# Two interleaved streams of one transformer program: their common order read from a table of runs

## What is computed

```python
x = L0_attn_hidden                                   # (4, 1024, 128)
x = layernorm(x + attn(x))          # global latent attention, then local attention, 16 heads of 8, 4 kv heads
x = layernorm(x + moe(x))           # 8 experts 128 -> 512 -> 128 (gelu), softmax gate, the 2 best
x = layernorm(x + linear_attn(x))   # elu + 1 feature maps of 64, running sum over the tokens
x = layernorm(x + local_layers(x))  # 2 layers: windows of 64 keys with 8 heads of 64, then a gated ffn (gelu)

# attn
x = x + global_latent_attn(rmsnorm(x, norm1_w), ...)   # rope and q/k norm, causal softmax over 1024
x = x + local_gqa_attn(rmsnorm(x, norm2_w), ...)       # window of 32

# local_layers, twice
h = shift_token(x); q, k, v = split(h @ wqkv)
q, k = rotary_xpos(l2norm(q) * qs, l2norm(k) * ks)
x = x + local_attention(q, k, v) @ wo
h = layernorm(shift_token(x)) * lg + lb
a, g = split(h @ w1 + b1); x = x + (a * gelu(g)) @ w2 + b2
```

## Time and profile before

| | us |
|---|---|
| median of 3 runs | 2644.71 |
| lowest, highest | 2635.4, 2645.03 |
| profiled execution | 2645.18 |
| its span | 2643.1 |
| mean granted clock of PE | 0.845 |

### The profile page before, as it was taken

How to read it: one execution, slowest core, us unless ns; L and a number is a source line. 1 busy time by engine, 2 the same in 40 slices (tenths; PEclk the granted TensorE clock), 3 DMA queues, 4 the chain that set the end, 5 groups by cost and what they waited for, 6 DMA issues and landing times.

```text
span 2643.1 us, 38819 instructions
## 1 busy us (share of the span) xinstructions
PE 2017.8 (76%) x14843; PEld 1256.7 (48%) x14843; DVE 1314.4 (50%) x2660; ACT 1241.3 (47%) x2610; POOL 592.8 (22%) x505
## 2 busy tenths in 40 slices
PE   2865986489867987679868976788757999758776
PEld 1123664244344755333545754442345666535454
DVE  4134225654366145445654157734665545467574
ACT  2642421376644331667543333566645565235453
POOL 0420000263311001235400011433510221024231
PEclk8776995698978986888888987888978999778998
DMA  3000000000000100000000000000100110000000
GB/s 112 1 1 1 25 25 1 10 16 10 25 5 17 41 13 5 5 13 17 25 14 16 33 9 9 13 5 17 33 5 5 33 33 17 0 20 21 13 17 13
DMA packets 32059, 45.50 MB, mean 17 GB/s; under 512 B 7824, under 2 KB 18948, under 8 KB 31748
## 3 DMA queue, kind: packets, MB, share of 16 engines
q1 hardware_dynamic: 31875, 43.01, 6.0%
HBM read 24.12 MB, written 2.10 MB: 10 GB/s over the span
## 4 chain that ended last, share of the span: by engine, by line
PE 53%; DVE 25%; ACT 10%; issue 7%; POOL 4%; SPq 1%; DVEq 0%; DMA 0%; ACTq 0%; POOLq 0%
PE PH L933 8%; PE PD L893 8%; PE PH L716 5%; PE PB L1082 4%; PE PB L1102 4%; PE PB L1018 3%; ACT back_arena L1345 2%; PE PD L760 2%; PE PB L1039 2%; PE PB L1138 2%; POOL front_arena L1936 2%; ACT front_arena L1213 2%; DVE back_arena L1818 2%; DVE back_arena L1817 1%; PE PB L1029 1%
## 5 line engine op out<-in xcount | busy, mean ns | idle before, releaser
L1973 POOL TENSOR_TENSOR back_arena<-back_arena 128x512 f32<-128x512 f32 x128 | 165.4, 1294 | 1052.3 <-DVE back_arena L1818 1052.2
L1213 ACT ACTIVATE front_arena<-PD 128x1024 f32<-128x1024 f32 (+3 forms) x384 | 303.3, 817 | 160.7 <-PE PD L760 159.0
L1302 ACT ACTIVATE front_arena<-PD,b 128x512 f32<-128x512 f32 x256 | 161.6, 683 | 260.6 <-PE PD L893 260.4
L933 PEld LDWEIGHTS PH<-W,front_arena 128*128 128x128 f32 x2048 | 248.2, 192 | 65.6 <-issue 34.1
L1936 POOL TENSOR_TENSOR front_arena<-front_arena,tri 128x256 f32<-128x256 f32 x256 | 201.1, 798 | 322.4 <-ACT front_arena L1213 321.6
L933 PE MATMUL PH<-W,front_arena 128*128 128x128 f32 x2048 | 255.3, 276 | 7.6 <-DVE R L1664 6.7
L1082 PE MATMUL PB<-wqkv,hT 128*128 128x512 f32 x384 | 233.1, 696 | 32.5 <-DVE back_arena L1818 12.7
L893 PE MATMUL PD<-xT,W 128*128 128x512 f32 x512 | 246.4, 605 | 1.2 <-ACT xT L1196 1.2
L716 PE MATMUL PH<-front_arena 128*32 128x512 f32 (+3 forms) x1536 | 189.4, 569 | 66.2 <-POOL front_arena L1936 41.5
L1825 DVE TENSOR_REDUCE fnm<-PB 128x4 f32<-128x512 f32 x128 | 88.3, 691 | 303.6 <-PE PB L1102 302.0
L1345 ACT ACTIVATE back_arena<-PB,fnm 128x128 f32<-128x128 f32 x512 | 180.9, 371 | 111.0 <-DVE fnm L1825 110.8
(11 more groups left out here) (241 smaller groups left out, 3398.0 us busy)
## 6 DMA issues: line engine op xcount, KB each, us to landing
W<-in_W SPq DMA_DIRECT2D x32, 512.0 KB, 3.4
back_arena<-back_arena SPq DMA_DIRECT2D x128, 128.0 KB, 2.3
X<-in_L_attn_hidden SPq DMA_DIRECT2D x64, 32.0 KB, 1.8
out_y<-Nb SPq DMA_DIRECT2D x64, 32.0 KB, 1.6
wqkv<-in_L_ffn_wqkv SPq DMA_DIRECT2D x1, 1536.0 KB
back_arena<-in_c_xpos SPq DMA_DIRECT2D x1, 1024.0 KB
back_arena<-in_L_ffn_w SPq DMA_DIRECT2D x1, 682.0 KB
wo<-in_L_ffn_wo SPq DMA_DIRECT2D x1, 512.0 KB
```

The lines of the kernel that those rows point to most:

```text
L933: ins = pe.matmul(p[:, 128 * t:128 * t + 128], hv[:, c, 128 * t:128 * t + 128], W12[e % WRING][:, HF + 128 * c:HF + 128 * c + 128], start= ...
L1213: act.activation(pb[:, :, 0:n], p[:, :, 0:n], ACT.Exp, scale=INV_SQRT_HD).then_inc(freed(b, "S", half, g, kc, jp), 1)
L1973: pool.tensor_tensor(T1[k % 2][:, hs, :], T1[k % 2][:, hs, :], T2[:, hs, :], ALU.add).then_inc(sg("rot"), 1)
```

## The change

The plan in `order()` is replaced by a table of run lengths, `RUNS`: 601 numbers for front, back, front and so on in turn, whose sums are the same 4 x 282 and 4 x 211 steps. The numbers were found offline by a search over the instructions and waits of the whole program. The estimates in the labels are no longer read. The first number is 283 and the last 223: front 0 is followed by one step of front 1 before back 0 starts, and the last 12 steps of back 2 stand ahead of back 3. The second edit puts `link(ins)`, which belongs to the last rotation product of `rope`, ahead of the yield of `qn` 0 instead of behind it.

```diff
--- before.py
+++ after.py
@@ -251,47 +251,28 @@
 assert len(F_AT) == len(FRONT) and len(B_AT) == len(BACK)
 
 
+RUNS = """
+283 1 8 2 3 1 3 1 2 1 3 2 3 1 4 1 9 1 1 1 2 1 4 1 10 1 1 2 2 2 1 1 1 3 2 2 1 1 1 7 2 2 2 1 1 4 1 1 1 1 1 3 1 5 2 5 3 1 1 1 1 1 1 2 1 16 2 1 1 2 1 2 1
...
+1 1 1 1 1 1 1 1 223
+"""
+
+
 def order():
 
-    streams = {"F": FRONT, "B": BACK}
-    left = {who: [sum(c[1] for _, c in labels[i:]) for i in range(len(labels))] for who, labels in streams.items()}
-    at, ready, out = {"F": 0, "B": 0}, {"F": 0.0, "B": 0.0}, []
-    pe = act = dve = 0.0
-    front_ends, taken = {}, {}
-    while at["F"] < B * len(FRONT) or at["B"] < B * len(BACK):
-        options = []
-        for who, labels in streams.items():
-            b, i = divmod(at[who], len(labels))
-            if b == B:
-                continue
-            start = ready[who]
-            if who == "B" and i == 0:
-                if b not in front_ends:
-                    continue
-                start = max(start, front_ends[b])
-            if who == "F" and i == 0 and b >= 2:
-                if b - 2 not in taken:
-                    continue
-                start = max(start, taken[b - 2])
-            (p, _, a, v) = labels[i][1]
-            start = max(start, pe if p else 0, act - 3, dve - 3)
-            behind = left[who][i] + (B - 1 - b) * left[who][0] + (left["B"][0] if who == "F" else 0)
-            options.append((start, -behind, who))
-        soonest = min(o[0] for o in options)
-        start, _, who = min((o for o in options if o[0] <= soonest + 0.05), key=lambda o: o[1])
-        b, i = divmod(at[who], len(streams[who]))
-        p, d, a, v = streams[who][i][1]
-        out.append((who, at[who]))
-        at[who] += 1
-        ready[who] = start + d
-        if p:
-            pe = start + p
-        act = max(act, start + p) + a if a else act
-        dve = max(dve, start + p) + v if v else dve
-        if who == "F" and i == len(FRONT) - 1:
-            front_ends[b] = ready[who]
-        if who == "B" and i == 0:
-            taken[b] = ready[who]
+    at, out = {"F": 0, "B": 0}, []
+    for n, run in enumerate(RUNS.split()):
+        who = "FB"[n % 2]
+        for _ in range(int(run)):
+            out.append((who, at[who]))
+            at[who] += 1
+    assert at == {"F": B * len(FRONT), "B": B * len(BACK)}, at
     return out
 
 
@@ -1533,8 +1514,8 @@
                         for s in range(2):
                             ins = dve.tensor_tensor(tmp[:, t, :, :, s], sw[:, t, :, :, 1 - s],
                                                     rope[a][:, t, 1:2, :].rearrange("p o (d s) -> p o d s", s=2)[:, :, :, s].to_broadcast([128, nh, HD // 2]), ALU.mult)
+                    link(ins)
                     yield front_at(b, "qn", a, 0)
-                    link(ins)
                     link(dve.tensor_tensor(QR, QR, arena_rope, ALU.add))
                     link(dve.tensor_tensor(arena_rope, QR, QR, ALU.mult))
                     yield front_at(b, "qn", a, 1)
```

## The result

| | before | after |
|---|---|---|
| median | 2644.87 | 2604.17 |
| lowest, highest | 2635.4, 2645.21 | 2595.42, 2604.94 |
| profiled execution | 2645.18 | 2595.42 |
| its span | 2643.1 | 2593.5 |
| mean granted clock of PE | 0.845 | 0.846 |

The ratio is 0.9847, interval [0.9817, 0.9877]: 41 us faster. Measured again beside other kernels the medians were 2598.65 and 2650.05, ratio 0.9804 [0.9785, 0.9823], 51 us. So 40 to 50 us is the size, and the forecast had 18.

The account below looks back on a forecast made before the run. Only the 1874 us middle, where PE idles 387 us, could change; DVE's strand limits the chain windows. 2645.2 - 5 (chain windows) - 8 (tables) - 5 (single waits) = 2627 us; ends 2607 to 2665, case range 2610 to 2644.

Parts of the forecast that it names:

- The middle part: Fronts 1 to 3 beside backs 0 to 2, 1874 us before: forecast some 1856, wrong if outside 1839 to 1873.
- The ends: Front 0 alone (467 us) and back 3 alone (302 us): same steps in both orders, so unchanged.
- The chain windows, what arrives: Last projection to `qT` (L854): some 58 back steps arrive, three windows grow by 47.6 (DVE alone) to 74 us.
- The chain windows, what leaves: Those 58 steps leave places costing 0.98 us each, 57 us; net of arrivals -5, ends -9 and +17.
- The tables: ScalarE's table loads fall from 82 to 69, 16.7 us of ACT; half taken, -8, bounds 0 and -17.
- Single waits: Waits outside the chain windows, such as before `nF` and `toT`, change: together -5 us, ends -12 and +3.
- The link: `link(ins)` above the yield makes DVE wait for the last rotation product: eight times nothing, at most 3 us.
- Unmixing: Rival: back steps in runs of four or more cost up to 1.28 us against 0.98 mixed; 2675 us, chance 0.18.
- Small waits go too: Rival: the new order also removes uncounted PE waits, such as at L716 behind the masks; 2575 us, chance 0.27.

Follow-up runs that it names:

- smooth_att: The changed kernel with back steps spread evenly in the six halves of global attention, hidden layers in one piece; 2642.6 us, 0.9991 of before.
- undo_dg: The changed kernel with the old order in the two pieces bringing 46 back steps into fronts 2 and 3's local chain windows; 2610.44 us, 0.9856 of before.
- tables_only: The old order with `link(ins)` moved and each back hidden layer's steps drawn together, 67 table loads instead of 82; 2658.57 us, 1.0051 of before.
- coarse: The new order's number of back steps between some 50 marks, spread evenly between them; 2689.8 us, 1.0162 of before.
- the filled kernels: The changed and the old kernel with PE's long idle pieces filled to the end by 857 and 1080 constant products; 2568.42 and 2599.74 us.
- part_a: The old order with `link(ins)` moved and the new order only from front 1's `toT` to its first local scores; 2637.86 us, 0.998 of before.
- part_bc: Old order, `link(ins)` moved, new order only from front 1's first local scores to half 1 of front 2's global attention; 2624.82 us, 0.9937 of before.
- part_dg: Old order, `link(ins)` moved, new order only in two pieces, from fronts 2 and 3's global attention into their local layers; 2644.19 us, 0.9991 of before.
- link_only: The old order with only the `link(ins)` line moved; 2642.76 us, 0.9988 of before.
- the two filled versions of before: The old kernel with constant products in PE's idle pieces: 773 (0.7 of each piece), 2636.27 us; 1080 (to the end), 2599.74 us.
- after_warm: The changed kernel with 641 products of a constant filling 0.7 of each long PE idle piece; 2593.85 us, 0.9779 of before.
- after_again: The changed kernel measured once more, nothing altered; 2598.65 us, 0.9804 of before.

## Why the prediction was right or wrong

Forecast 2627, measured 2604 and 2599: the direction and the range held, the size didn't. The middle part was to be between 1839 and 1873 us; it is 1820.7, so by its own test the forecast was wrong. **The step that failed** is the price of what leaves global attention: the mean of 0.98 us a step, with the places of the steps that stay put at nothing. Attention became 79.4 us shorter for 54 steps fewer, 1.47 each, and 48 of these us go when the same counts are spread evenly (smooth_att: 15 us of idle time, 33 us of PE busy longer at a lower clock). Step by step:

- **The ends.** Right in their order, wrong in "unchanged": back 3 alone took 307.3 instead of 299.1 us with the same instructions.
- **The chain windows, what arrives.** Right. Three windows were to get 58 steps and grow by 47.6 (DVE alone) to 74 us. They grew from 35.9, 38.6 and 38.3 to 44.1, 63.4 and 51.8, by 46.5: DVE's bound, 0.80 us a step. The forecast's -5 had taken 52 us, 0.90 a step. Idle time before `qT` was to fall under 8 us in fronts 2 and 3 local: it is 13.0 and 2.7. The other three windows changed by -12, +10 and -10 us.
- **The chain windows, what leaves.** This step failed. I priced a step that leaves attention at the *mean* of 0.92 to 1.04 us, and so had -57 against +48 to +55. In the whole order the six windows and the three attentions together became 45.0 us shorter (34.4 - 79.4). undo_dg shows what the two pieces did: 60 steps left attention and 67.3 us with them, 1.12 each (1.44 in front 2, 0.91 in front 3), and 53.7 us came elsewhere, 0.90 each. For this part alone, with 46 of the term's 58 steps, the term of -5 measures -6 to -14, mostly outside its end of -9. So the mean was not far off for these pieces; the large price belongs to the whole order with its places.
- **The tables.** The term of -8 has no run behind it. tables_only, with two loads fewer than the new order has, gained nothing up to the cut, but its drawn-together steps brought waits of their own, so a term of this size is neither shown nor excluded. The earlier trace rows showed ACT as the pacing engine of one 15 us stretch; that was no evidence for the rest. The count of loads that I read out of the order was right: ACT has 2610 instructions before and 2597 after, 13 fewer. The estimate of -17 that I had worked out from the Trainium skill, "ScalarE: Activation LUTs", section "What ACT_TABLE_LOAD costs", has no run behind it either. For 15 loads less ACT's busy time fell by 20.2 us in tables_only, 1.35 each, so the second half of the page's 2.66 us shows neither there nor as idle time.
- **Single waits.** The term was -5 with an end at -12. Behind the rms norms alone (N) the wait fell from 36.5 to 14.5 us, and before `nF` from 27.8 to 14.2. I had counted the steps that now stand ahead of such a wait and gone through single places, and missed the two longest, 11.4 us before front 2's `toT` (now 3.6) and 12.0 before front 3's (now 3.5). The `toT` waits behind X did stay, as I had argued.
- **The link** was priced at nothing and gave 0.9988 [0.9977, 0.9998]. SP and POOL never appear as what the new order waits for more.
- **Unmixing** did not come: the waits before the back's values and the score tiles rose by 25 us in sum, which may be its trace, and 94 us of other waits in the lists above went. smooth_att speaks against it: with the runs of back steps in attention spread evenly the kernel is 38 us slower, where this rival had 5 to 15 us faster.
- **Small waits go too.** Its number, 2575, is no further off than mine (29 and 24 us against 23 and 28), but its mechanism did not happen. The wait at the masks fell from 31.8 to 23.2 only, and the idle time that is neither before `qT` nor before a `toT` rose by some 10 us (211 to 221). What went were the long pieces that I had counted too low.
- **What no step had.** PE's busy time as a function of the order. The forecast priced idle time and counts and took busy time as given, though the earlier trace rows shows a clock of 0.77 where front 0 idles a third of the time. At the same work PE was busy for 33 us more in smooth_att's attention (14 more in coarse's), and the filled kernels show that a long idle piece has a second price, paid by the work behind it: 10 to 27 us of the gain.

What stays open: *why* the even places inside attention let the clock fall. smooth_att's attention has more pieces of 0.8 us and more (45 against 27, 79 us against 45), and they go with a lower clock, but I tried no kernel that changes such short pieces alone. What the fewer table loads bring by themselves stays open too. Nor was an order tried in which counts alone change and each place stays fine.

## What to carry to other kernels

When steps move between two streams, don't price them at the mean of the stretch that they leave: measure what one step less saves there and one more costs where it goes, by a kernel with one piece of the order undone. Where an order was searched, don't keep its counts and spread them evenly: here the fine places were worth 86 us against even ones, about half in attention and half outside it, and the even order was slower than the old one. If PE's idle pieces of several microseconds can't be filled with real work, fill them to the very end with products that nobody reads: 30 us here on top of the new order, 5 us where the last third was left idle.

## What the runs showed of the hardware

The stretch behind front 3's last product has the same instructions in the same order in all kernels here. It took 342 to 346 us in before, part_a, part_bc, part_dg, link_only, the two filled versions of before and after_warm, and 350 to 354 in the others, the changed kernel among them (342.2 in before, 354.2 in tables_only and 351.6 in the changed kernel in the fences above), with nearly the same idle time (94 to 98 us). What differs is the clock, 0.86 against 0.83, and busy time, 246 to 249 against 253 to 259 us. after_warm and after_again differ only in the added products ahead of it, and took 345.9 and 351.6 us. So when the level falls depends on more than the work of the stretch itself, and an edit's time can be off by some 10 us for that alone.

The same holds inside the middle. Front 3's local layer from `qT` to `toT 2`, in the traces of after and of after_again, which are the same kernel:

```profile
1882.10:1962.50 80.40, 70.46 (x801) 50.31 (x802) 58.28 (x101) 47.82 (x133) 17.35 (x10) 0.86 0.05 11
```

```profile
1879.90:1970.20 90.30, 80.31 (x801) 55.72 (x802) 58.29 (x101) 47.87 (x133) 17.36 (x10) 0.75 0.05 10
```

It is the same 801 products with the same 10 us of idle time, and 9.9 us longer at the lower clock, the size of the distance between these two executions (2595.42 and 2605.51 us). What decides between the two, no run here shows.
